# Two-layer graph network, one core: the place of VectorE's x1 tile and pooled scaling in a dense step, and ScalarE's add of one

## The reference

```
pooled = relu(LN((x[src] * (1 + softplus(c) * w_edge)) @ pool_w + pool_b) * g_p + b_p)
agg    = max(segment_max(pooled, dst), 0)
x1     = LN(x + relu(LN([x, agg] @ final_w + final_b) * g_f + b_f))      # first layer
feat   = [mean over edges of comp[type] x x1[src] (8 bases), x1]
out    = LN(x1 + feat @ weight + bias)                                   # second layer
```

## Time and profile before

| | |
|---|---|
| median of three timed runs | 920.42 us |
| span of the profiled execution, first to last instruction | 1001.7 us |
| time of the profiled execution outside its span | none is shown |
| VectorE busy over the span | 802.6 us (80%) |
| TensorE, ScalarE, GpSimd busy over the span | 821.0, 622.5, 662.4 us |
| granted TensorE clock, mean over the span | 0.929 |
| dense stage (98 steps) | up to about 510 us of the span |

### The profile page before, as it was taken

How to read it: one execution, slowest core, us unless ns; L and a number is a source line. 1 busy time by engine, 2 the same in 40 slices (tenths; PEclk the granted TensorE clock), 3 DMA queues, 4 the chain that set the end, 5 groups by cost and what they waited for, 6 DMA issues and landing times. The chain is left out here.

```text
span 1001.7 us, 18559 instructions
## 1 busy us (share of the span) xinstructions
PE 821.0 (82%) x4588; PEld 589.6 (59%) x4588; DVE 802.6 (80%) x2823; ACT 622.5 (62%) x2862; POOL 662.4 (66%) x702
## 2 busy tenths in 40 slices
PE   5889999999999999999997777674687887888790
PEld 3677777777777777777786666463343433443340
DVE  6989999999999999999997677553377774776891
ACT  4799999999999999999996555555001111111121
POOL 2667777777777777777756646466756666667544
PEclk9899999999999999999999898987789898888895
DMA  4466575655655556556552122241466676666640
GB/s 114 127 220 216 189 224 196 202 196 192 203 193 192 191 193 202 201 199 202 199 183 88 63 61 69 72 187 41 139 246 238 234 242 229 209 217 249 204 157 28
DMA packets 88575, 175.46 MB, mean 175 GB/s; under 512 B 16715, under 2 KB 34023, under 8 KB 82198
## 3 DMA queue, kind: packets, MB, share of 16 engines
q1 hardware_dynamic: 71286, 144.02, 42.5%
q0 software_dynamic: 15744, 29.71, 9.9%
q10 hardware_dynamic: 1440, 0.56, 0.2%
HBM read 105.88 MB, written 70.88 MB: 176 GB/s over the span
## 5 line engine op out<-in xcount | busy, mean ns | idle before, releaser
L704 ACT ACTIVATE junk<-ps 128x128 bf16<-128x128 f32 x884 | 234.8, 295 | 48.0 <-remote 18.1
L656 PE MATMUL ps<-agg_all,w_cen 128*128 128x512 f32 (+1 forms) x400 | 197.0, 648 | 38.9 <-DVE agg_all L1177 26.4
L704 ACT ACTIVATION_READ_ACCUMULATOR junk<-ps 128x1 f32 x884 | 196.6, 227 | 0.0
L436 POOL TENSOR_TENSOR work<-work,vec_raw 128x512 f32<-128x512 f32 x98 | 124.4, 1269 | 87.0 <-DVE work L1078 86.3
L551 PE MATMUL ps<-w_cen,xT 128*128 128x128 f32 x984 | 164.2, 300 | 0.0
L656 PEld LDWEIGHTS ps<-agg_all,w_cen 128*128 128x128 f32 x400 | 82.1, 211 | 138.0 <-issue 137.7
L806 ACT ACTIVATE st<-st 128x4 f32<-128x4 f32 x25 | 5.1, 206 | 235.2 <-issue 122.3
L551 PEld LDWEIGHTS ps<-w_cen,xT 128*128 128x128 f32 x984 | 133.3, 201 | 29.9 <-issue 29.9
L406 POOL DMA_INDIRECT x_table<-agg_all,scat_i x98 | 102.3, 1044 | 73.2 <-ACT agg_all L744 32.2
L1177 DVE TENSOR_TENSOR agg_all<-coefs,ps 128x1024 f32<-128x1024 f32 x98 | 117.4, 1209 | 39.4 <-PE ps L642 19.6
L524 PE MATMUL ps<-w_cen,work 128*128 128x128 f32 x984 | 137.0, 284 | 2.0 <-ACT y_root L730 1.5
(11 more groups left out here) (139 smaller groups left out, 1445.8 us busy)
## 6 DMA issues: line engine op xcount, KB each, us to landing
coefs<-coef_line SPq DMA_DIRECT2D x49, 1024.0 KB
rows<-in_x SPq DMA_DIRECT2D x97, 256.0 KB
x_table<-work SPq DMA_DIRECT2D x97, 256.0 KB
out_rows<-outb SPq DMA_DIRECT2D x97, 256.0 KB
x_dst_table<-x_dst SPq DMA_DIRECT2D x98, 64.0 KB
rows<-x_dst_table SPq DMA_DIRECT2D x24, 256.0 KB
same_prev<-mask_line SPq DMA_DIRECT2D x7, 224.0 KB, 4.2
x_dst<-in_x,dst_i POOLq DMA_INDIRECT x98
```

The costliest lines, as they stand in the source:

```text
L436: pool.tensor_tensor(h, h, vec_raw[:, BET_F:BET_F + 1, :].broadcast_to([P, CH, D]), ALU.add).then_inc(S["pool_b"], 1)
L656: last = pe.matmul(MT[b][:, 0:n * D], w_cen[:, W_BASE + m, :], prod[:, b, m, 0:n, :].rearrange("p t d -> p (t d)"), start=(m == 0), stop=( ...
L704: last = nc.scalar.activation(junk[:, kind * CH + m, :], bank[:, cols(m, m + 1)], ACT.Square, accum_out=power[:, b, 1, TOP + kind * CH + m ...
```

## The change

On ScalarE, `turned` uses `nc.scalar.add` with the immediate 1.0 in place of an Identity activation whose bias is a column of ones in SBUF. On VectorE, the pooled scaling becomes a function of its own (`pooled_scaled`), `scaled` takes the tiles that it is to do, and the dense order becomes: scan before the second `bn_stats`; three scalings; the x1 tile; the fourth scaling; the third `bn_stats`; the pooled scaling; the fourth `bn_stats`; the output product. The other order stays as it was (pooled scaling, then four scalings). `residual` becomes a function, called in the same place.

```diff
--- before.py
+++ after.py
@@ -709,8 +709,7 @@
                     if is_group(c, 5):
                         act.wait_ge(S["pe_c"], s - 4)
                         need(act, S["pe_d"], s - 6)
-                        nc.scalar.activation(x1T[:, 1 - b, :, :].rearrange("p c d -> p (c d)"), VT, ACT.Identity,
-                                             bias=one[:, 0:1]).then_inc(S["act_c"], 1)
+                        nc.scalar.add(x1T[:, 1 - b, :, :].rearrange("p c d -> p (c d)"), VT, 1.0).then_inc(S["act_c"], 1)
 
                 def roots():
                     if 2 <= c <= GROUPS + 3:
@@ -1022,12 +1021,17 @@
                         dve.wait_ge(S["dve_m"], min(s - 4, GROUPS))
                     first = moments(RES, TOP, 1 - b)
                     read_at = own.count
-                if fresh:
-                    if is_dense(c, 3):
-                        dve.wait_ge(S["pool_b"], s - 2)
-                    h = hn[:, (c - 3) % SLOTS, :, :].rearrange("p c d -> p (c d)")
-                    dve.scalar_tensor_tensor(h, h, 0.0, rows[:, (c - 3) % SLOTS, 0:CH, :].rearrange("p c d -> p (c d)"),
-                                             ALU.max, ALU.add).then_inc(S["dve_v"], 1)
+
+                def residual():
+                    if fresh:
+                        if is_dense(c, 3):
+                            dve.wait_ge(S["pool_b"], s - 2)
+                        h = hn[:, (c - 3) % SLOTS, :, :].rearrange("p c d -> p (c d)")
+                        dve.scalar_tensor_tensor(h, h, 0.0,
+                                                 rows[:, (c - 3) % SLOTS, 0:CH, :].rearrange("p c d -> p (c d)"),
+                                                 ALU.max, ALU.add).then_inc(S["dve_v"], 1)
+
+                residual()
                 if stats:
                     own.need(first)
                     spread_at = spread(RES, TOP)
@@ -1068,19 +1072,22 @@
                         dve.scalar_tensor_tensor(st[:, 3, TOP:TOP + CH], power[:, 1 - b, 0, RES:TOP], -0.5, st[:, 7, RES:TOP],
                                                  ALU.mult, ALU.mult).then_inc(S["dve_m"], 1)
 
-                def scaled():
+                def pooled_scaled():
                     if is_tile(c, 2):
                         need(dve, S["pe_cp"], s - LATE - 3)
                         dve.scalar_tensor_tensor(pooled[:, b, :], HE, st[:, 7, EDG:EDG + 1],
                                                  vec_raw[:, GAM_P, :], ALU.mult, ALU.mult).then_inc(S["dve_te"], 1)
+
+                def scaled(tiles=range(CH)):
                     if is_group(c, 2):
-                        for m in range(CH):
+                        for m in tiles:
                             last = dve.scalar_tensor_tensor(hn[:, (c - 2) % SLOTS, m, :], H[b][:, cols(m, m + 1)],
                                                             st[:, 7, TOP + m:TOP + m + 1], vec_raw[:, GAM_F, :],
                                                             ALU.mult, ALU.mult)
                             if m < CH - 1:
                                 own.mark(last)
-                        last.then_inc(S["dve_t"], 1)
+                            else:
+                                last.then_inc(S["dve_t"], 1)
 
                 def dense_out():
                     if is_dense(c, 7):
@@ -1125,14 +1132,16 @@
                     residual_ready()
                     stats_of(0)
                     inverses(at)
+                    scanned()
                     stats_of(1)
-                    scanned()
                     means()
-                    scaled()
+                    scaled(range(3))
+                    first_layer()
+                    scaled(range(3, CH))
                     stats_of(2)
+                    pooled_scaled()
                     stats_of(3)
                     dense_out()
-                    first_layer()
                     edge_beta_added()
                 else:
                     residual_ready()
```

## The result

The changed kernel takes 913.33 us (median of four runs, 912.58 to 915.03) against 920.85: 0.9912 of before, interval 0.989 to 0.9935. By the medians that is 7.5 us less, by the ratio 8.1 (6.0 to 10.1 by its interval), where 16 were forecast; 913.3 is inside the stated range. The kernel before took about 921 us on three occasions and 993 on another, for a reason that was not found (the chip had the number 7 in the one of 993 and in one of 921), and the profile shown ahead of the prediction (span 1001.7) is like the 993, the changed kernel's (span 912.1) like the 921.

The account below looks back on a forecast made before the run. VectorE was taken to set the 4.92 us step, and the beta addition L436 the new 4.73. 98 dense steps x 0.19 = 18.6 us, less 1.7 and 1 for stalls, gain 16: 920.4 becomes 904.5 us, range 892 to 917.

Parts of the forecast that it names:

- What bounds before, and what the x1 tile costs in L436's shadow: Dense stage: VectorE sets the 4.92 us step; the x1 tile beside GpSimd's beta addition costs 0.52 us, moved 0.26.
- L994 pays nothing at the end of L436: VectorE's moments, starting 0.19 us before GpSimd's beta addition ends, were charged no wait.
- rival 2: The block holds VectorE's moments until the beta addition ends: step 4.85, gain 7 us, 913.5; chance 0.15.
- The hand-over from L436 to the residual: From GpSimd's beta addition to VectorE's residual: taken as 0.08 us, making the step 3.30 + 0.08 + 1.27 + 0.08 = 4.73.
- rival 1: GpSimd's hand-over to the residual is slow: near 0.27 gain 0, at 0.22 gain 5 us, 915.5; chance 0.10.
- The idle gap before L1029 released by L436: Sign of the forecast: VectorE idles a little before the residual until GpSimd's beta addition ends.
- The round through the pooled scaling: Pooled scaling through TensorE, ScalarE's L712 and VectorE's L1068 back to the pooled scaling: 4.65 us, under the 4.73 step.
- Both fit under 4.73, barely: The pooled scaling's ring, 4.65 us, and TensorE's own round, 4.62, stay below the forecast step; without ScalarE's saving the ring is 4.76.
- Rival 3: TensorE waits for the pooled scaling, hand-overs costing over 0.27 us more: at step 5.00, +8 us, 928; chance 0.08.
- ScalarE's copy saves 0.11 and is off the path: L712 as an immediate add saves 0.11 us; off the path, but keeps ScalarE at 4.58 and the ring at 4.65.
- L427 does not slide into the x1 tile's new place: Earlier x1 stores ease GpSimd's 18 x_dst waits (13.0 us), so L427 should not run beside the moved x1 tile.
- The sum: 98 dense steps x 0.19 = 18.6 us, less 1.7 for stalls and 1 more: gain 16 us, 904.5.

Follow-up runs that it names:

- first_small: Changed kernel with the pooled scaling back ahead of the scalings and GpSimd's L427 cut to one column; 917.69 us against 921.2, 0.9959 of before.
- pooled_next: Changed kernel with the pooled scaling one place earlier, right behind the fourth scaling; 962.22 us against 993.38, 0.9707 of before.
- x1_last: Changed kernel with the x1 tile back at the end, behind the output product, pooled scaling kept behind the third stats; 905.87 us against 921.2, 0.9826.
- identity_small: Changed kernel with ScalarE's Identity activation restored and GpSimd's L427 cut to one column; 915.02 us against 920.91, 0.9955 of before.
- again_2: The kernel before, unchanged, profiled again on an occasion of 920.91 us; span 922.8 us, average step 4.93.
- pooled_next_2: Changed kernel with the pooled scaling right behind the fourth scaling, timed again on another occasion; 900.14 us against 921.2, 0.9767 of before.

## Why the prediction was off, step by step

- **What bounds before, and what the x1 tile costs in L436's shadow**: right. It fell from 605 to 349 ns.
- **L994 pays nothing at the end of L436** (against the Trainium skill's rule as worded, rival 2): nearly right. L993 in the changed kernel starts 0.19 before L436's end, is recorded for 0.22 in place of 0.15, and holds VectorE 0.07 longer. The 913.5 us that rival 2 gave came out, but by luck: its step was 4.85 and its cause another. The same wait is large where the moments start earlier, 0.33 us in `first_small`.
- **The hand-over from L436 to the residual**, bounded by 0.01 and 0.27 and taken as 0.08: it is at most 0.03 to 0.04 (L1030 at 453.14, L436's end at 453.10), and rival 1 falls. The round through the beta addition is 4.68, and 4.94 was met exactly where 0.26 was added to it. What links L436's end to the residual stays open: the wait on `pool_b`, or the moments that L436 holds, which L1030 follows by 0.09 in the changed kernel (453.05 to 453.14) and in `first_small` (351.47 to 351.56) alike. The idle gap before L1029 released by L436, which the prediction named as a sign, is in no waits view.
- **The round through the pooled scaling, 4.65**: this is the step that failed. I led it from L574 over the turned x1 tile (L513) to L712 and put ScalarE's work between them at nothing (P is the pooled scaling's start, as in the prediction). But ScalarE's queue has L755, the square of the pooled row, ahead of L765 and L712, and L755 waits for L574 too. So L712 starts at P+2.49, not at P+2.32: after L574, 0.27 of L754 and 0.57 of L764. The rest of my links held (L567 at P+0.39 for 0.43, L719's end to L1072 0.03 for 0.08). The round is 4.81 and not 4.65, above every other limit. `pooled_next` (0.20 out of the round, 0.07 of it left over), `x1_last` (0.26 out, 0.10 left over) and `identity_small` (0.09 in) all fit 4.81. No run moved L755 itself out of the way. "Both fit under 4.73, barely" named the thin place; its price was 0.16 short. Rival 3 had this round with 0.27 as the point from which it makes the kernel slower; it reached the path without reaching that point.
- **ScalarE's copy saves 0.11 and is off the path**: the size was nearly right (L712 holds ScalarE 0.49 in place of 0.59, and the steps differ by 0.09), the place wrong. It is on the path.
- **L427 does not slide into the x1 tile's new place**: false. From the residual to L427 is 2.21 us before (449.46 to 451.67) and 2.89 after (453.14 to 456.03), because the gather L406 starts 0.24 later against the residual and lasts 0.46 longer. L427 runs beside the x1 tile, the sign of being wrong that the prediction named. That the x1 tile still costs 0.26 is luck: it starts 0.07 ahead, and L427 pays. As soon as the step is 0.10 longer, the x1 tile pays.
- **The scan ahead of the second stats** costs nothing: not tried by itself.
- **The sum**: 0.19 a step was 0.10 (4.91 to 4.81), which over 98 steps is 9.8; the average steps, 4.93 and 4.84, make it 8.8, and the dense stage ended 8.4 us earlier. The timed gain is 7.5 to 8.1. The loss per stall in my sum was read from a profile of the kind of the 993 us and mattered little.

## What to carry to other kernels

When an instruction is moved later, list every instruction that waits for it on each engine, and then what is queued behind each of those: the forgotten link was not the one that consumes the value, but one that stands ahead of the next engine's other work. Where several rounds lie within 0.2 us of each other, work out each to the end, and try the neighbouring places too: one place earlier for one 0.26 us instruction was worth 13 us on top of the 8 of the whole change. Two instructions that exclude each other should be given a distance larger than the jitter of the step, not just an order.

## What was unexpected of the hardware

- A gather issued by GpSimd is slowed beside VectorE's residual. L406 takes 1.04 us where it starts before the residual (454.25 against 454.38) or long after it (`x1_last`, 353.11), and 1.50 where the residual started 0.11 before it (453.14, 453.25). Means: 1068 ns in `again_2`, 1489 in the changed kernel, 1481 in `pooled_next_2`. In between it depends on the distance alone, as two places in `again_2` show:

```profile
381.75 0.68 DVE L1029 SCALAR_TENSOR_TENSOR work<-work,rows 128x512 f32<-128x512 f32 x1
...
382.02 1.32 POOL L406 DMA_INDIRECT x_dst<-in_x,dst_i  x1 [0.50 <-DMA x_dst_table<-x_dst]
...
451.09 0.68 DVE L1029 SCALAR_TENSOR_TENSOR work<-work,rows 128x512 f32<-128x512 f32 x1
...
451.57 1.12 POOL L406 DMA_INDIRECT x_dst<-in_x,dst_i  x1 [0.70 <-DMA x_dst_table<-x_dst]
```

  Both gathers end 1.59 to 1.60 us after the residual's start (383.34, 452.69), and the 1.50 of the changed kernel at 1.61: each time as if its 1.04 had begun some 0.12 before the residual's end. The residual has two SBUF inputs. The Trainium skill (SBUF — State Buffer, "Who interferes with whom") has two such inputs hold off a GpSimd instruction that reads SBUF, and its remark that descriptor generation needs only the write interface is given there as inferred; the 0.45 us here fit a gather that reads its index column. That reading was not tested: no run took away one of the residual's inputs.
- Which of the two pays depends on who starts first: L427 ahead by 0.02 us costs VectorE 0.21 on the x1 tile (0.47 held for 0.26), the x1 tile ahead by 0.07 costs GpSimd 0.11 on L427. The changed kernel, 0.07 from the edge, has steps of 4.81 and a few of 5.1, and hardly any between. The lock is not all there is to those few: with L427 cut they are still 4.91 to 5.14, at the same places of the span.
